# Layer 3 attention: the value products of an older pair of tiles regrouped between the score units on TensorE

## What is computed

```python
s = jnp.einsum('bhid,bhjd->bhij', q * scale, k)
gm = jax.lax.stop_gradient(jnp.max(s, axis=-1, keepdims=True))
causal_mask = jnp.triu(jnp.ones((N, N), bool), 1)
p = jnp.where(causal_mask, 0.0, jnp.exp(s - gm))
num = jnp.einsum('bhij,bhjd->bhid', p, v)
out = num / (jnp.sum(p, axis=-1, keepdims=True) + EPS)
out = out.transpose(0, 2, 1, 3).reshape(B, N, H * Dh)
return out @ Wo + bo
```

## Time and profile before

| | |
|---|---|
| median of 3 runs | 1985.29 us (1982.64 to 1988.27) |
| profiled execution | 1990.92 us, its span 1989.1 us |
| busy share of the span | PE 87%, PEld 56%, DVE 71%, ACT 60%, POOL 56% |
| attention of layer 3 | from about 1000 us to the end of the span |

### The profile page before, as it was taken

How to read it: one execution, slowest core, us unless ns; L and a number is a source line. 1 busy time by engine, 2 the same in 40 slices (tenths; PEclk the granted TensorE clock), 3 DMA queues, 4 the chain that set the end, 5 groups by cost and what they waited for, 6 DMA issues and landing times. The chain is left out here.

```text
span 1989.1 us, 30683 instructions
## 1 busy us (share of the span) xinstructions
PE 1724.1 (87%) x10623; PEld 1107.6 (56%) x10623; DVE 1417.5 (71%) x2088; ACT 1201.9 (60%) x2047; POOL 1121.0 (56%) x1025
## 2 busy tenths in 40 slices
PE   6738999999878798968789998998999999999988
PEld 2416777789543476624635555555555555555564
DVE  3756777763455898753278888888888888888883
ACT  5573333346436576443378787777777777877760
POOL 2425555523200674113237888788888878888880
PEclk7668999997789999988899999999999999999999
DMA  1303222221100000004119998999998999999992
GB/s 39 84 21 94 68 82 86 83 67 32 27 14 6 8 1 1 1 23 138 48 32 158 158 157 158 161 160 161 162 161 150 156 154 161 168 164 165 160 162 54
DMA packets 632582, 193.21 MB, mean 97 GB/s; under 512 B 591617, under 2 KB 624146, under 8 KB 632414
## 3 DMA queue, kind: packets, MB, share of 16 engines
q1 hardware_dynamic: 624038, 167.69, 46.7%
q0 software_dynamic: 8224, 23.51, 3.9%
q10 hardware_dynamic: 168, 0.06, 0.0%
HBM read 36.96 MB, written 12.55 MB: 25 GB/s over the span
## 5 line engine op out<-in xcount | busy, mean ns | idle before, releaser
L2883 DVE TENSOR_REDUCE half_max<-scores 128x1 f32<-128x1024 f32 x512 | 614.6, 1218 | 134.4 <-PE scores L2665 128.6
L2582 POOL TENSOR_TENSOR p_low<-p,p_high 128x2048 f16<-128x2048 f32 (+15 forms) x256 | 576.1, 2251 | 152.7 <-ACT p_high L2809 131.4
L2665 PE MATMUL scores<-k_high,q_pair 128*128 128x512 f16 x1024 | 304.6, 379 | 67.6 <-ACT p L2794 63.0
L2794 ACT ACTIVATE p<-scores,exp_bias 128x1024 f32<-128x1024 f32 (+7 forms) x384 | 317.4, 861 | 70.7 <-DVE exp_bias L2888 68.3
L2809 ACT ACTIVATE p_high<-p 128x2048 f16<-128x2048 f32 (+15 forms) x256 | 282.6, 1104 | 40.7 <-DMA pT_high<-p_high 32.4
L2665 PE MATMUL scores<-k_low,q_pair 128*128 128x512 f16 x1024 | 304.9, 379 | 0.0
L2685 PEld LDWEIGHTS scores<-v_pair,pT_high 128*128 128x128 f16 x2176 | 150.5, 98 | 102.6 <-issue 61.3
L2685 PE MATMUL scores<-v_pair,pT_low 128*128 128x129 f16 x2176 | 185.2, 221 | 10.8 <-DMA pT_low<-p_low 10.5
L2685 PE MATMUL scores<-v_pair,pT_high 128*128 128x129 f16 x2176 | 187.1, 221 | 3.5 <-DMA pT_high<-p_high 3.4
L2685 PEld LDWEIGHTS scores<-v_pair,pT_low 128*128 128x128 f16 x2176 | 146.2, 98 | 45.9 <-DMA pT_low<-p_low 14.9
L2665 PEld LDWEIGHTS scores<-k_low,q_pair 128*128 128x128 f16 x1024 | 99.2, 97 | 122.2 <-issue 0.8
(11 more groups left out here) (503 smaller groups left out, 3207.0 us busy)
## 6 DMA issues: line engine op xcount, KB each, us to landing
pT_high<-p_high SPq DMA_TRANSPOSE x256, 3.6
pT_low<-p_low SPq DMA_TRANSPOSE x256, 3.7
slots<-zero_row SPq DMA_DIRECT2D x1, 3036.0 KB, 14.3
slot_rows<-slots SPq DMA_DIRECT2D x23, 132.0 KB, 2.3
slots_out<-expert_out SPq DMA_DIRECT2D x23, 128.0 KB, 1.8
w_up<-in_L_ffn_inter_w_dram SPq DMA_DIRECT2D x1, 2048.0 KB
x_tokens<-in_L_attn_x_dram SPq DMA_DIRECT2D x4, 256.0 KB, 3.5
dispatched<-moe_rows SPq DMA_DIRECT2D x1, 1024.0 KB, 10.9
```

The costliest lines, as they stand in the source:

```text
L2582: pool.tensor_tensor(flat(pl[:, buf, b0:b0 + n, :]), flat(p32[:, buf, b0:b0 + n, :]), flat(ph[:, buf, b0:b0 + n, :]), ALU.subtract).then_i ...
L2665: mm = pe.matmul(ps[:, b.start + i, :], q, k[:, par, cs(2 * half + i)], start=start, stop=not start)
L2794: act.activation(flat(p32[:, buf, b0 + first:b0 + first + w, :]), flat(ps[:, banks(p, half), :])[:, 0:w * P], ACT.Exp, bias=bias[:, p:p + ...
L2883: dve.tensor_reduce(mx[:, p % 2, half:half + 1], flat(ps[:, b[half], :]), AX.X, ALU.max, negate=True)\
```

## The change

The thirds of the value products are placed by a table. Piece 0 stays behind the projection, and piece 1 follows it there. Piece 2, which stood behind S0, now stands where piece 1 was, between S1 and S0. Behind S0 there is none. A round is then: L1, L0, projection, piece 0, piece 1, S1, piece 2, S0. No instruction is added or removed, and the order inside the pieces, the other engines' programs and all waits are the same.

```diff
+                    PIECES = {(0, 0): (0, 1), (1, 1): (2,)}
+
                     def head(at, par, i, first, last):
                         for s in range(PAIRS):
                             for i in range(2):
...
                                     if (i, half) == (0, 0) and not last:
                                         unit_free(at, s)
                                         project(at, 1 - par, s, UBANK)
-                                    if (i, half) != (0, 1) and (not first or s >= LAG):
+                                    if (i, half) in PIECES and (not first or s >= LAG):
                                         now, v_par, pair = shift(at, par, s - LAG, PAIRS)
-                                        add_up(now, v_par, pair, 2 * i + 1 - half - 1, 3)
+                                        for piece in PIECES[i, half]:
+                                            add_up(now, v_par, pair, piece, 3)
                                     if last and half == 0:
                                         turn_next(BY_ROUND * s + i)
```

## The result

The median went from 1985.29 to 1996.76 us (five runs each, 1991.00 to 2000.98 after). The ratio is 1.0054, 95% interval 1.003 to 1.0078: slower by 11 us. The profiled execution of the changed kernel took 1997.17 us, with a span of 1995.4.

What follows compares the result with a forecast made beforehand. The prediction took SP's transpose queue and the projection-bank chain as bounds near 57.2 us a head. Heads 1 to 14 add 8.4, head 0 2.6, head 15 gives back 1: together +10 on 1985.3, so 1995, range 1985 to 2013.

Steps and rivals of the forecast that it cites:

- The chain: Loop low part, projection, PE's work before S0, S0, its maximum, low part: 6.44 us in round 6, predicted to become 7.11.
- hidden by piece 2: Piece 1 moved ahead of S1: S1 comes 0.65 us later, its reduction is over before S0 arrives, cost nothing.
- The two bounds of before: SP's queue issuing transposes and the chain through the one projection bank, both put within a per cent of 57.2 us a head.
- The pace of a head: Heads 1 to 14 go from 57.2 to 57.8 us, 14 x 0.6 = 8.4 us in all.
- allowance for loss: Two bounds of 57.2 and 57.3 us don't mesh without loss: 0.5 us a head, between 0 and 1.2.
- Round 4: The round with the denominators: S0 starts 4.29 us after the low part, new chain has it ready at 3.86; stays 7.53.
- Round 0: 8.45 us with ACT's 1.71 us transpose wait; new chain asks 6.99 plus 0.4 for a late projection, hence 7.4.
- The ends: Head 0, without a late queue, gains 2.6 us; head 15, without projection, gives back perhaps 1 of its transpose waits.
- SP's gap at a head's start closes: `summed` comes at least 0.86 us earlier, so SP's 0.2 us gap, where `turn_high` waits for it, closes.
- The queue alone: Rival: SP's queue alone sets the pace, the longer chain only takes up stalls; +3 us, 1988; chance 0.25.
- The stalls stay: Rival: ACT and PE wait as before, each round's addition comes on top; +35 us, 2020; chance 0.10.
- Faster: Rival: piece 2 costs the chain nothing and `summed` comes earlier; 3 to 10 us less, about 1978; chance 0.07.

## Why the prediction was right, and where it was not

**The chain.** Piece 2 enters it with 0.69 us. Predicted for rounds 1 to 3: 6.99, measured 7.00; for rounds 5 and 6: 7.11, measured 7.13 and 7.12; round 7 unchanged, 7.19 both times; S0 3.86 after the low part, measured 3.87. Piece 1 was put at nothing, "hidden by piece 2"; that is how it came out, and alone it cost no time either (0.9999), though there round 6 grew by 0.25.

**The two bounds of before.** The prediction calls both queue and chain "within a per cent" of 57.2. For the chain that was wrong, and by its own sum: the rounds add up to 54.77 (with 7.2 put for round 0), 4% less, and the run without loads shows them at 54.8. Only the lengthened rounds, at 57.3, stand beside the queue.

**The pace of a head.** Predicted 57.8, measured 57.76. The sum of the rounds was 57.3 and the allowance for loss 0.5; the rounds as measured exceed that sum by 0.44. But the reason given for the allowance was wrong. It was to come from transposes that arrive too late for pieces placed 0.86 us earlier. No wait for a transpose is left: the slack that the longer chain gave the queue was enough. The 0.44 is 0.27 in round 4, where the prediction held 7.53 for a floor, 0.12 in round 0 (7.52 in place of 7.4 in most heads), and 0.05 in the others. The size of the allowance was right by luck.

**Round 4**, the step that failed. "Stays 7.53" took the addition of 0.88 us for work that belongs to the round. The run with POOL's steps moved shows that only 0.17 of it is work and the rest a wait for POOL, 0.96 us in the changed kernel. Why it grew can be read from the traces (below, DVE and POOL in the kernel before). There the addition ran from 1512.00 to 1512.88 and met the end of a low part of POOL's, over at 1512.85; in the changed kernel POOL stands 1 us earlier in the round (its addition of the sums starts 0.26 us before the end of DVE's low part, before 0.72 behind it), and DVE meets that one nearly whole.

```profile
1512.00 0.88 DVE L2894 TENSOR_SCALAR den<-o_raw 128x16 f32<-128x16 f32 x1
```

```profile
1511.69 1.16 POOL L2582 TENSOR_TENSOR p_low<-p,p_high 128x512 f16<-128x512 f32 x1 [0.68 <-ACT p_high L2809]
1512.81 1.28 POOL L2565 TENSOR_TENSOR o_raw<-o_raw 128x512 f32<-128x512 f32 x1
```

That POOL is earlier because ACT's splits are no longer held up by `out` and by transposes is argued from the waits and was not tried apart. The prediction said that POOL's part would start sooner, and counted this as a gain.

**Round 0.** The wait of ACT for a transpose is gone as predicted (first and third line below: `out` and the widest split no longer wait), but another wait, 0.91 before, is longer. The exponentials of the small tile wait for DVE's bias (second line), and L0 of the next tile waits 1.19 for these (last line, PE). The chain asked for 6.99 plus what the projection is late; 0.4 was taken, within 0 to 0.9, and 0.52 is what came.

```profile
1484.78 0.38 ACT L2819 ACTIVATE o_raw<-scores 128x258 f32<-128x258 f32 x1
...
1486.60 0.37 ACT L2797 ACTIVATE p<-scores,exp_bias 128x128 f32<-128x128 f32 x1 [0.49 <-DVE exp_bias L2891]
1486.87 1.90 ACT L2812 ACTIVATE p_high<-p 128x2048 f16<-128x2048 f32 x1
```

```profile
1487.11 0.59 PE L2665 MATMUL scores<-k_high,q_pair 128*128 128x512 f16 x2 [1.19 <-ACT p L2797]
```

**The ends.** Head 0 was put at +2.6; with the half of head 1 that follows, 0.3 by the same step, that is 2.9, and 2.7 was measured. The last head was to give back 1; from the last denominators to the end it is 0.5 less, with half a head at the longer pace in it (0.3), so 0.8. The waits behind the last scores are 0.6 shorter (1.54 + 0.54 before, 0.97 + 0.53 after), but earlier in the last head the products wait longer for transposes than before (2.75 and 0.67, where it was 1.45). So the size of this term came out, and its reason is not shown.

**The queue.** "SP's gap at a head's start closes" was wrong: it opened, from 0.23 to 1.74 us. It was thought of as a wait for `summed`; with the chain in charge the queue waits for the whole loop, and the gap at a head's start is where that shows. The other statement, that the queue would show gaps, was the right one.

**The rivals.** *The queue alone* (1988): against it stand the gap above and the changed kernel without weight loads, at 1997.01. For the kernel before the same rival's picture was true: a queue without a gap was the bound, worth 27 us when four issues a head were taken from it. So what the Trainium skill says (page Perfetto Trace Analysis, section What "DMA-bound" means) of a sequencer track of solid slices holds for the first kernel; in the second the slices are still nearly solid and shortening the queue gives nothing, so the picture alone does not decide. With the addition's wait out of the way (1987.47), the time was that rival's, for another reason: the chain had been stretched to the length of the queue's pace, 57.1. *The stalls stay* (2020): the waits for transposes, which it is about, all went. *Faster*: it needed a chain below 6.6 a round; it is 7.0.

**The forecast**, 1995 with a range from 1985 to 2013, against 1996.76: the lengthened rounds were read rightly, and the margin over the queue, 0.6 a head, has the right size. But what fills that margin is the wait of one short addition, which the prediction did not see; without it a head takes 57.1, within 0.1 us of the queue's pace before, and the time does not change. That the forecast lies within 2 us of the measured time is therefore in part luck.

## What to carry to other kernels

Work moved in an engine's program is priced here by the loop that it enters and not by the engine's busy share: follow from one instance of a loop's step to the next and ask whether the moved work stands ahead of it. Where two bounds lie near each other, removing the one that does not bind gives nothing, and removing the other gives only what lies between the two (0 and 27 us before, 16 and 0 after); here the busy queue looked alike in both kernels, and the two were told apart by relieving each in turn. An instruction with one shape and more than one duration may be waiting for something that the profile doesn't count as a wait, so compare its duration where its neighbours are idle before it is put into a sum.

## What the runs showed of the hardware

DVE's addition of 128x16 values from SBUF to SBUF takes 0.17 us where POOL is idle (the run with POOL's steps moved; 163 to 167 ns in the kernel before with the low part earlier), and longer wherever it begins during a POOL instruction (816, 876 and 1131 ns at the median in three orders; in all runs 0.41 to 1.19 us, by how much of POOL's instruction is left). It then ends 0.02 to 0.04 us behind that instruction in every such case, and the profile counts it as busy the whole time. Not every DVE instruction waits so: the bias of a tile (128x1 values, also from SBUF to SBUF) took 211 to 215 ns each time in the kernel before, though about half of them lie wholly inside a POOL instruction (view by source line).

```profile
L2888 DVE TENSOR_SCALAR exp_bias<-half_max x216: 211/214/215, 1101.4 to 1868.7; 128x1 f32<-128x1 f32 x108
```

The Trainium skill (page SBUF — State Buffer, section SBUF: two separate sides) has VectorE and GpSimd sharing one pair of ports by an exclusive lock, held for a whole instruction, and VectorE taking it in its 2-port modes or with two inputs from SBUF; the trace agrees in what it shows, 0.17 against 1.13 us and an end together with POOL's. In which mode the addition runs, no run here shows.

Four small weight loads took ACT 2.4 us to issue in the head shown (1.08 + 1.31), and for 2.14 of them it computed nothing; leaving out the same four on SP shortened a head by 57.2 - 55.0 = 2.2 us.
